# Expert results stored as blocks by SyncE and collected by 64 indirect gathers, with the expert weights requested from ScalarE

## The reference

```python
tidx, tw = _gate(x, gate_w, gate_bias)          # 8 of 64 experts for each token, 4 of 8 groups
w_dense = zeros((T, E)).at[arange(T)[:, None], tidx].add(tw)
def body(acc, ws):
    wg, wu, wdn, cw = ws                        # wg, wu: 256 x 128, wdn: 128 x 256
    hmid = silu(x @ wg) * (x @ wu)
    return acc + cw[:, None] * (hmid @ wdn), None
y = scan(body, zeros_like(x), (We_gate, We_up, We_down, w_dense.T))
return y + silu(x @ Ws_gate) * (x @ Ws_up) @ Ws_down     # a shared expert
```

## Time and profile before

| | |
|---|---|
| runs | median of 3: 974.66 us (973.48 to 976.91) |
| the profiled execution | 967.33 us |
| its span, first to last instruction | 965.5 us |
| first gather of the tile loop starts | 653.4 us |
| last copy of a tile's result starts | 930.9 us |
| all scatters landed | 935.7 us |
| busy share of the span | PE 78%, DVE 48%, ACT 27%, POOL 28% |

### The profile page before, as it was taken

The page is one execution under the profiler, slowest core; times in us unless marked ns, Lnnn a source line. Parts: engine busy times, 40 slices in busy tenths (PEclk is TensorE's granted clock), DMA queues, the critical chain, the costliest instruction groups (busy, mean ns, idle before and its releaser), DMA issues. The chain is left out here.

```text
span 965.5 us, 19279 instructions
## 1 busy us (share of the span) xinstructions
PE 751.2 (78%) x6571; PEld 494.0 (51%) x6571; DVE 464.4 (48%) x1279; ACT 259.9 (27%) x520; POOL 271.1 (28%) x306
## 2 busy tenths in 40 slices
PE   5799999776659989889987789655667767665646
PEld 4455656455444546465447677534445545542315
DVE  4423335766736222233665886887523323222216
ACT  1121213744612211122454411341111111111150
POOL 1020002002502100000043551315566565564420
PEclk9999999988869999997995558977987887788878
DMA  8999991100985999911983200107666666568868
GB/s 331 383 372 380 417 404 62 51 1 2 332 286 221 352 390 408 396 61 31 193 189 87 69 5 1 44 1 238 194 200 194 192 197 191 186 184 260 262 213 322
DMA packets 70781, 200.40 MB, mean 208 GB/s; under 512 B 11912, under 2 KB 37744, under 8 KB 64944
## 3 DMA queue, kind: packets, MB, share of 16 engines
q1 hardware_dynamic: 60720, 176.29, 53.0%
q0 software_dynamic: 7680, 20.98, 6.9%
q10 hardware_dynamic: 2304, 2.10, 0.7%
HBM read 185.51 MB, written 13.83 MB: 206 GB/s over the span
## 5 line engine op out<-in xcount | busy, mean ns | idle before, releaser
L1989 PE MATMUL ps<-moe_wset,moe_xgT 128*128 128x256 f32 (+1 forms) x320 | 106.1, 464 | 57.2 <-DVE moe_xgT L2080 22.1
L2123 POOL DMA_INDIRECT moe_xg<-xn_rows,moe_idx x80 | 79.4, 992 | 106.1 <-DVE moe_idx L2071 68.4
L1989 PEld LDWEIGHTS ps<-moe_wset,moe_xgT 128*128 128x128 f32 (+1 forms) x320 | 62.9, 219 | 75.2 <-issue 48.2
L2132 POOL DMA_INDIRECT y_rows<-moe_ysb,moe_row x80 | 79.4, 993 | 35.9 <-issue 24.1
L2085 DVE TENSOR_TENSOR moe_hrow<-moe_hs,ps 128x128 f32<-128x128 f32 x80 | 22.9, 286 | 105.7 <-ACT moe_hs L2107 66.8
L2107 ACT ACTIVATE moe_hs<-ps 128x128 f32<-128x128 f32 x80 | 22.3, 278 | 174.3 <-PE ps L1989 86.3
L1469 POOL TENSOR_TENSOR ss_dec<-ss_dec,ss_cT 128x256 f32<-128x256 f32 x48 | 39.9, 869 | 93.5 <-ACT ss_dec L1424 51.0
L2080 DVE COPY moe_xgT<-ps 128x256 f32<-128x256 f32 x80 | 33.9, 424 | 63.4 <-remote 38.9
L2004 PE MATMUL ps<-moe_wset,moe_hT 128*128 128x256 f32 (+1 forms) x160 | 58.4, 453 | 2.4 <-DVE moe_hT L2090 1.6
L1282 PE MATMUL ps<-xnT,w_win 128*128 128x512 f32 x128 | 58.3, 614 | 0.0
L1314 PE MATMUL ps<-ss_dec 64*64 64x32 f32 (+2 forms) x1792 | 46.5, 255 | 11.5 <-issue 9.6
(11 more groups left out here) (401 smaller groups left out, 1412.3 us busy)
## 6 DMA issues: line engine op xcount, KB each, us to landing
x0ctxT<-ctx_T SPq DMA_DIRECT2D x8, 3202.0 KB, 19.2
x1ctxT<-ctx_T SPq DMA_DIRECT2D x8, 3202.0 KB, 13.8
x0ctxN<-ctx SPq DMA_DIRECT2D x8, 3072.0 KB
x1ctxN<-ctx SPq DMA_DIRECT2D x8, 3072.0 KB
moe_wset<-moe_gate_up SPq DMA_DIRECT2D x80, 256.0 KB
moe_wset<-L_ffn_We_down SPq DMA_DIRECT2D x80, 128.0 KB
moe_yg<-y_rows SPq DMA_DIRECT2D x7, 1024.0 KB, 11.0
ss_dec<-seg_rows SPq DMA_DIRECT2D x8, 768.0 KB, 17.0
```

The source lines that it names most:

```text
L1989: mm = pe.matmul(ps[c * n_:(c + 1) * n_, 2 + a2, 0:2 * FE], xgT[:, a2, h, c * n_:(c + 1) * n_], src[:, aw, h, :], start=h == 0, stop=h == ...
L2123: nc.gpsimd.indirect_dma_start(out=xg[:, a4, :], out_offset=None, in_=xn_rows, in_offset=bass.IndirectOffsetOnAxis(ap=idx[:, a4:a4 + 1], a ...
L2132: nc.gpsimd.indirect_dma_start(out=y_rows, out_offset=bass.IndirectOffsetOnAxis(ap=row[:, a4:a4 + 1], axis=0), in_=ysb[:, a4, :], in_offse ...
```

## The change

What the diff does, part by part:

- **First block.** The code of the choice (`order8`, `marked[:, u, 1]`, `rowt`) goes. PE now makes the token group's number in three further products, of the bits of j: 96 more matmuls, all of 104 columns instead of 208. The table `idxt` comes from four DVE instructions. SP fills rows 40 x 128 to 104 x 128 of `y_rows` with `xn` (8 DMAs of 1 MB), which gives rows that no tile writes a value.
- **Tile loop.** POOL only gathers. SP stores each tile's result as one block of 128 rows at n x 128 (a plain DMA). ACT takes over the reading of the expert number and the requests for the weights, behind its copy (8 tiles behind) and its SiLU (4 behind). The lags of PE grow from 0, 1, 2, 3 to 0, 2, 4, 6, those of DVE likewise; `xg`, `idx`, `ysb` get 8 buffers, the products in SBUF 4. The choice weights leave DVE's list here.
- **Collecting.** `y_rows` is in the order of tiles, so POOL gathers the results of 128 tokens for one choice at a time, by `sloti`: 8 groups x 8 choices = 64 indirect DMAs. DVE works out the choice weights first and then adds up all 8 groups, 64 instructions. The diagonal matrices and the matmuls on them go.

```diff
             with nc.Block(no_gpsimd_drain=True) as block:
                 @block.sync
                 def _(sp):
                     sp.dma_start(xn_rows.rearrange("(j p) d -> p j d", p=P), xn[:]).then_inc(s_rows, 16)
+                    for first in range(LEAST_TILES, MOST_TILES, NT):
+                        sp.dma_start(y_rows[first * P:(first + NT) * P, :].rearrange("(j p) d -> p j d", p=P), xn[:]).then_inc(s_spare, 16)
...
-                            mm = pe.matmul(ps[:, 4, 0:2 * MOST_TILES], in_tile[:, j % 2, k // 2, :, k % 2], marked[:, j % 2, :, k // 2, :, k % 2],
-                                           start=j + k == 0, stop=j == NT - 1 and k == 7)
+                            mm = pe.matmul(ps[:, 4, 0:MOST_TILES], in_tile[:, j % 2, k // 2, :, k % 2], marked[:, j % 2, k // 2, :, k % 2],
+                                           start=first and j == 0, stop=last and j == NT - 1)
+                            for x in range(3):
+                                if j >> x & 1:
+                                    mm = pe.matmul(ps[:, 5 + x, 0:MOST_TILES], in_tile[:, j % 2, k // 2, :, k % 2],
+                                                   of_tile[:, j % 2, k // 2, :, k % 2], start=first and j == 1 << x, stop=last and j == NT - 1)
...
-                        dve.drain()
-                        nc.vector.tensor_tensor(marked[:, u, 1], of_tile[:, u], pairs_of(order8[:, j * 8:(j + 1) * 8], MOST_TILES), ALU.mult).then_inc(s_oh, 1)
...
-            xg = ring("xg", [P, 4, D])
+            xg = ring("xg", [P, RING, D])
...
+                @block.scalar
+                def _(act):
+                    LEAD = 4
+                    def step(n, m, g, live, pairs):
+                        lag = LEAD + DOWN - GU
+                        if live(lag):
+                            k, a8, b = n - lag, (m - lag) % RING, (m - lag) % 2
+                            act.wait_ge(s_dn, k + 1)
+                            if not early(k):
+                                act.wait_ge(s_ys[a8], turn_of(g, m, lag) * 16)
+                            nc.scalar.copy(ysb[:, a8, :], ps[:, 4 + b, 0:D]).then_inc(s_yc, 1)
+                        lag = LEAD
+                        if live(lag):
+                            k, a4, b = n - lag, (m - lag) % 4, (m - lag) % 2
+                            act.wait_ge(s_gu, k + 1)
+                            wait(act, s_hh, k - 3)
+                            nc.scalar.activation(silu[:, a4, :], ps[:, 2 + b, 0:P], ACT.Silu).then_inc(s_si, 1)
+                        if pairs:
+                            load(n, m, pairs)
...
+                @block.sync
+                def _(sp):
+                    def step(n, m, g, live):
+                        sp.wait_ge(s_yc, n + 1)
+                        sp.dma_start(y_rows[ds(n * P, P), :], ysb[:, m, :]).then_inc(s_ys[m], 16)
+                    sp.wait_ge(s_spare, (MOST_TILES - LEAST_TILES) // NT * 16)
+                    run(sp, step, 0)
...
+                @block.gpsimd
+                def _(pool):
+                    for j in range(NT):
+                        for k in range(8):
+                            nc.gpsimd.indirect_dma_start(out=yg[:, j, k * D:(k + 1) * D], out_offset=None, in_=y_rows[0:MOST_TILES * P, :],
+                                                         in_offset=bass.IndirectOffsetOnAxis(ap=sloti[:, 0, j, k:k + 1], axis=0)
+                                                         ).then_inc(collected(j, k), 16)
...
-                    for m in range(4):
-                        sp.wait_ge(s_ys[m], rounds * (RING // 4 * 16))
                     for j in range(NT):
-                        src = y_rows[P * P + j * 8 * P:P * P + (j + 1) * 8 * P, :].rearrange("(p k) d -> p (k d)", k=8)
-                        if j < NT - 1:
-                            sp.dma_start(yg[:, j, :], src).then_inc(s_yg[j], 16)
...
+                            ins = nc.vector.scalar_tensor_tensor(xt[:, j, :], y[:, k, :], w8[:, j, k:k + 1], xt[:, j, :], ALU.mult, ALU.add)
```

More of the change, by code:

```diff
@@ L1934, in experts @@
             s_yc = sem("tile_result_copied")
-            s_ys = [sem(f"tile_stored{m}") for m in range(4)]
+            s_ys = [sem(f"tile_stored{m}") for m in range(RING)]
             PEEL = 16
+            GU, TURN, DOWN, AHEAD = 2, 4, 6, 6
             def whole_rounds(eng):
@@ L2003, in down @@
                         for c, src in enumerate((wset,) if late is None else (wset, wset2)):
[L2004 removed]
+                            mm = pe.matmul(ps[c * n_:(c + 1) * n_, 4 + b, 0:D], hidT[:, a4, c * n_:(c + 1) * n_], src[:, a8, 2, :],
                                            start=True, stop=True)
@@ new lines, in _, with step @@
+                @block.sync
+                def _(sp):
+                    def step(n, m, g, live):
+                        sp.wait_ge(s_yc, n + 1)
+                        sp.dma_start(y_rows[ds(n * P, P), :], ysb[:, m, :]).then_inc(s_ys[m], 16)
+                    sp.wait_ge(s_spare, (MOST_TILES - LEAST_TILES) // NT * 16)
+                    run(sp, step, 0)
+            rings.close()
+            yg = own("yg", [P, NT, 8 * D])
+            s_yg = [sem(f"moe_collected{r}") for r in range(NT)]
@@ new lines, in experts, with collected, _ @@
+            s_yl = [sem(f"moe_collected_last_{x}") for x in ("middle", "one")]
+            s_ya = sem("moe_result_added")
+            def collected(j, k):
+                return s_yg[j] if j < NT - 1 or k < 4 else s_yl[k // 7]
+            with nc.Block(no_gpsimd_drain=True) as block:
+                @block.gpsimd
+                def _(pool):
+                    for j in range(NT):
[3 more added lines that the diff above has]
+                                                         ).then_inc(collected(j, k), 16)
+                @block.scalar
+                def _(act):
+                    for j in range(NT):
+                        act.wait_ge(s_ya, j + 1)
+                        act.dma_start(out.rearrange("(j b) s d -> j (b s) d", b=2)[j], xt[:, j, :]).then_inc(s_out, 16)
+                    act.wait_ge(s_out, 16 * NT)
```

317 lines of the change are left out of this document (114 added, 203 removed).

## The result

The changed kernel takes 946.25 us (median of 4 runs, 943.42 to 948.25) against 974.07 of the kernel before beside it: 0.972 of it, 95% interval 0.967 to 0.977. I had forecast 980 us. Eight of the 34 us between forecast and result come from no stage: I put the median of the runs 7.3 us above the profiled execution, as it stood for the kernel before, and for the changed kernel the profiled execution (946.9) is 0.65 above the median.

A forecast was written before the change was run, and what follows sets the result against it. GpSimd's two indirect DMAs (2.57 us a tile) plus stalls of unknown cause were taken to bound the loop. First block -4, whole tiles -54, halves +2, drain +2, collecting +59 gave +5: 974.66 to 980 us, range 956 to 1012.

The forecast's parts named there:

- The whole tiles: Tile loop, 64 whole tiles: from 3.24 to 2.4 us each with ScalarE as the bound, a gain of 54 us.
- rival 1: Faster loop: ScalarE's queue runs ahead, loop meets DMA engines at 2.15 us a tile, halves 4.0, total 960; chance 0.27.
- The stalls: Tile loop: waits about every four tiles, cause unknown, taken to vanish; nothing won if scatters are not involved.
- Rival 2: Tile loop: stalls stay, caused also by gathers and weight loads; 3.0 us a tile, +38 us, total 1018; chance 0.13.
- Halves: The 15 tiles of halves: 4.25 instead of 4.1 us each, a loss of 2 us, between -4 and +6.
- Start: First block, ahead of the tile loop: 4 us earlier, between 1 and 6.
- drain: End of the tile loop: draining six steps instead of three costs 2 us more.
- From execution to median: Whole kernel: the median of the runs put 7.3 us above the profiled execution.
- Tail: Collecting after the last copy: 93 us with 64 gathers on GpSimd, 59 more than before.
- slow tail: Collecting: the 64 gathers run at 1.5 us each beside VectorE's additions, +13 us, total 993; chance 0.15.
- The test that I named: Signs in the new profile: loop gain over 60 us means faster; TensorE or DMA full while ScalarE waits means wrong.

The follow-up runs named there:

- e5: Changed kernel with both cuts, fewer gate and up weight bytes loaded and half of the gate and up contraction left out: 944.0 us, one run.
- e6: Changed kernel with expert reads and weight requests moved from ScalarE to SyncE, which also stores results: 975.73 us, 1.009 of the kernel before.
- e11: Changed kernel with weight requests shared, ScalarE asking for gate and up, SyncE for down: 942.43 us, 0.969 of the kernel before.
- e3: Changed kernel with most gate and up transfers cut from 512 to 64 columns, 416 instead of 640 KB a tile: 939.3 us, one run.
- e1: Changed kernel's loop with the scatter put back, 13 tiles behind the gather, and the old collection: 977.91 us, 1.002 of the kernel before.
- e2: Changed kernel with the old lags (1, 2, 3, 3 tiles), 8 buffers kept: 948.81 us, 0.971 of the kernel before.
- e8: e1 with gathers replaced by plain loads by SyncE, so the scatter is GpSimd's only indirect DMA a tile: 894.88 us, one run.
- e7: Changed kernel with every tile's gather issued twice, the second into a buffer nobody reads: 1032.79 us, one run.
- e10: e7 with the second gather only for odd tiles, 1.5 indirect DMAs a tile on average: 988.18 us, one run.
- e14: e1 with a GpSimd memset of 128 x 512 behind each scatter as a pause: 957.59 us, one run.
- e9: e7 with the second gather fetching rows of 64 bytes instead of 1 KB: 1040.73 us, one run.
- e17: e14 with half the pause, a memset of 128 x 256: 973.37 us, 0.999 of the kernel before.
- e18: e14 with a quarter of the pause, a memset of 128 x 128: 979.71 us, 1.008 of the kernel before.

## Why the prediction was wrong

- **The whole tiles: the step that failed.** "ACT is the new bound at 2.25. ... I take 2.4 us: the 2.25, and 0.15 for waits." The step that failed is this sum, 1.60 + 0.65: I added the compute of 0.65 us to the queue's 1.60. That ACT's list is a bound was right as far as the runs go: e5 has it left when bytes and matmuls are cut, and e6 shows a list as the bound again; e11 adds that a second bound stands close to it. The rows of ACT show that SiLU runs while the queue reads the next expert; list and waits came to 1.81 us in the rows shown and 2.01 on average. The term was -54 and measured -74. My own row had the other reading ("1.60 if the queue works ahead of the engine"), and I filed it under rival 1 with a chance of 0.27. The first half of that rival came true, a queue ahead of its compute, at 2.08 instead of its 2.15 and with halves at 3.75 instead of 4.0, which made its 960 another 4.5 and 4 us too high. Its second half, that the loop then meets the DMA engines, did not: with a third of the bytes gone the pace is 2.06 (e3).
- **The stalls.** "Should the stalls have nothing to do with scatters" stood at my upper bound, and the forecast took them to vanish. They did, and e1, e2 and e8 show that the missing second indirect DMA did it; lags and buffers were of little account, and the move of the requests kept SP's list from becoming the next bound (e6). That I let the stalls vanish was in part luck: I wrote "I don't know the cause". e7 to e10 show that it is how many indirect DMAs GpSimd issues, not their direction or bytes. That "none needs to follow another so closely" was right for the changed kernel; 1.5 a tile, still in bursts, cost 0.7 us (e10), and a pause between pairs won time back (e14). Rival 2 had one thing right, gathers do it too (e7), and its price wrong: one indirect DMA a tile brought no stall.
- **Halves.** Forecast +2, measured -5.2. The same mistake: I took 4.25 us, between the 3.86 of SP's list and 4.51 with the compute on top; the compute overlaps, and ACT's list came to 3.62 in the rows shown. e11 confirms that the list was the bound (3.29 when shared).
- **Start.** Forecast -4, measured 0. The first block took 44.8 us to its first gather before and after; over all profiles the new one is some 2 us shorter, so that 4 was too much. The longer lag, which I had counted only at the other end, as +2 of drain (1.8), costs 1 to 2 us here.
- **From execution to median.** I added 7.3 us for the distance between the profiled execution and the median, a property of one execution, not of the kernel; measured -0.65.
- **Tail.** Forecast +59, measured +56.3; 63 spacings took 81.7 us where I had 81.0 and 4 for contention. Most are 1.25 us, not 1.286, and ten of the 64 gathers were longer than 1 us, 3.0 us in all, against my 4. The "slow tail" rival, in which every addition costs a gather 0.26 us, did not come. By the rule that I weighed (Trainium skill, SBUF — State Buffer, "Who interferes with whom") a VectorE instruction with two SBUF inputs contends with a GpSimd instruction that reads SBUF. Here the trace agrees at times: of 16 gathers beside the choice weights five took 1.23 to 1.44 us, and of 30 beside additions, which have two SBUF inputs, five took 1.14 to 1.19; five additions took 0.52 to 0.55 us instead of 0.48. The others kept their 0.94 to 0.95. The first two of the long gathers below start 0.07 and 0.18 us behind a weight step of DVE, the third within a row of eight additions.

```profile
859.10 0.69 DVE L2156 TENSOR_TENSOR moe_pick<-moe_slot,moe_slots 128x512 f32<-128x512 f32 x1
...
864.49 0.69 DVE L2158 TENSOR_TENSOR moe_pick<-moe_pick,moe_cwt 128x512 f32<-128x512 f32 x1
...
920.90 4.39 DVE L2172 SCALAR_TENSOR_TENSOR xt<-moe_yg,moe_w,xt 128x256 f32<-128x256 f32 x8 [5.49 <-DMA moe_yg<-y_rows,moe_sloti]
```

```profile
859.17 1.44 POOL L2129 DMA_INDIRECT moe_yg<-y_rows,moe_sloti  x1 [0.30 <-issue]
...
864.67 1.34 POOL L2129 DMA_INDIRECT moe_yg<-y_rows,moe_sloti  x1 [0.30 <-issue]
...
924.40 1.16 POOL L2129 DMA_INDIRECT moe_yg<-y_rows,moe_sloti  x1 [0.30 <-issue]
```

- **The test that I named.** "If the gain of the loop is over 60 us, the kernel is faster." It was 79, and it is. "I am wrong on the loop if PE or the DMA engines are full there and ACT waits": both read as nearly full, and e3 to e5 show that this sign was a poor one: neither was what the loop waited for.

What stays open: by what path GpSimd's indirect DMAs hold up the signals and queues of others, and whether it is their issuing or their row transfers. The runs show that they do, how much, and that a long enough pause shortens it (one run). Open too is what holds the whole tiles of e11 at 2.08.

## What to carry to other kernels

The queue of an engine and its compute are two lists side by side: do not add them up, but add to the queue's only the waits that stand in it (here 1.81 us for lists of 1.60 and 0.65). Near a balance of several resources cut two or three at once to find the bound, for a busy share of 90 or 98% proves nothing by itself. Count indirect DMAs: in this loop, with tight signals between engines, the second one a tile cost 1.3 us of pace (3.41 against 2.08). Scattering in the loop cost 64 x 1.31 = 84 us in the whole tiles (e1), and 64 gathers at the end, where nobody else signals, 53 us more of tail (90.5 against 37.0 in e1): they were the cheaper place.

## What the runs showed of the hardware

- Indirect DMAs issued by GpSimd hold up others: with 1, 1.5 and 2 a tile the pace was 2.08, 2.79, 3.41 us (the changed kernel, e10, e7). With rows of 64 bytes it was 3.52 (e9). Single waits of ScalarE and VectorE without a visible releaser reached 13.3 us.
- A memset of 543 ns on GpSimd behind each pair gave 13 to 20 us back (one run of e14 against e1's fastest and median); memsets of half and a quarter of the columns gave nothing clear of the noise (e17, e18).
- Of 64 gathers in a row 54 ran at 1.25 us each, 0.94 to 0.95 of it busy, the 0.30 between them always there. The ten others were busy 1.14 to 1.44 us, all beside VectorE instructions with two SBUF inputs.
- ScalarE's queue with one expert reading and two requests takes 1.81 us a tile beside 0.65 us of compute; SyncE's with a store in addition 2.34 us (e6).
- With both queues reading the expert and one indirect DMA a tile (e11), single readings took up to 762 ns, where 266 is usual.
